# Two test-time-training/FFN layers on one core: rates turned on chip, the scan's first input and weights loaded a stage earlier, one FFN trip and one base product moved

## What is computed

```python
def step(carry, x):                       # scanned over 32 chunks of 16 tokens
    W1_s, b1_s = carry                    # one 16x16 state per head and sequence
    xq, xk, xv, eta_mb = x
    Z1 = xk @ W1_s + b1_s
    grad = _ln_fused_l2_bwd(Z1, xv - xk, ln_w, ln_b)
    Attn1 = jnp.tril(xq @ xk.swapaxes(-1, -2))
    b1_bar = b1_s - jnp.tril(eta_mb) @ grad
    Z1_bar = xq @ W1_s - eta_mb * Attn1 @ grad + b1_bar
    last_eta = eta_mb[:, :, -1, :, None]
    W1_new = W1_s - (last_eta * xk).swapaxes(-1, -2) @ grad
    b1_new = b1_s - jnp.sum(last_eta * grad, axis=-2, keepdims=True)
    out = xq + _ln(Z1_bar, ln_w, ln_b)
    return ((W1_new, b1_new), out)
...
ttt_lr_eta = jax.nn.sigmoid(ttt_lr).transpose(0, 1, 2, 4, 3) / HD      # the learning rates
...
hdn = jax.nn.silu((xf @ gate_w.T) * gate_s) * ((xf @ up_w.T) * up_s)   # the FFN, 512 -> 1408 -> 512
out = (hdn @ down_w.T) * down_s
```

## Time and profile before

| what | value |
|---|---|
| median of 3 runs | 2010.04 us (2007.79 to 2011.96) |
| profiled execution, its own time | 2006.43 us |
| its span, first to last instruction | 2004.8 us |
| mean granted TensorE clock | 0.981 |
| TensorE busy (PE) | 1875.6 us, 94% |
| VectorE, ScalarE, GpSimd busy | 1224.2, 979.8, 1022.7 us |

### The profile page before, as it was taken

How to read it: one execution, slowest core, us unless ns; L and a number is a source line. 1 busy time by engine, 2 the same in 40 slices (tenths; PEclk the granted TensorE clock), 3 DMA queues, 4 the chain that set the end, 5 groups by cost and what they waited for, 6 DMA issues and landing times. The chain is left out here.

```text
span 2004.8 us, 34531 instructions
## 1 busy us (share of the span) xinstructions
PE 1875.6 (94%) x12504; PEld 1414.9 (71%) x12504; DVE 1224.2 (61%) x2415; ACT 979.8 (49%) x2115; POOL 1022.7 (51%) x894
## 2 busy tenths in 40 slices
PE   5898999998999999799999989999999999999998
PEld 3676777666666665488778866777777777777776
DVE  4563566788788874467344456666666666666663
ACT  3332556566665655445444335444444444444442
POOL 5444566556565654420243347555555555555552
PEclk9899999999999999989999999999999999999999
DMA  7785657436334533232789841222323233322320
GB/s 243 275 297 191 230 169 262 123 110 220 119 114 150 190 117 97 73 108 92 239 258 289 290 176 54 88 113 95 123 99 116 95 105 117 116 83 73 107 98 30
DMA packets 157111, 297.96 MB, mean 149 GB/s; under 512 B 20240, under 2 KB 97296, under 8 KB 150288
## 3 DMA queue, kind: packets, MB, share of 16 engines
q1 hardware_dynamic: 155856, 294.70, 43.7%
q10 hardware_dynamic: 1088, 1.05, 0.2%
HBM read 221.52 MB, written 74.19 MB: 148 GB/s over the span
## 5 line engine op out<-in xcount | busy, mean ns | idle before, releaser
L2005 POOL TENSOR_SCALAR probs<-probs,rsum 128x512 f32<-128x512 f32 x256 | 396.1, 1565 | 249.0 <-DVE rsum L2141 249.0
L2105 ACT ACTIVATE p_tok<-bank 128x512 fp32r<-128x512 f32 x256 | 154.5, 606 | 346.4 <-PE bank L2045 346.3
L2137 DVE TENSOR_REDUCE nmax<-bank 128x1 f32<-128x512 f32 x256 | 158.9, 683 | 95.2 <-PE bank L2037 95.2
L2147 DVE TENSOR_TENSOR p_tok<-bank,p_tok 128x512 fp32r<-128x512 f32 x256 | 173.3, 680 | 16.1 <-ACT p_tok L2105 16.1
L2097 ACT ACTIVATE probs<-bank,nmax 128x512 f32<-128x512 f32 x256 | 172.8, 692 | 3.2 <-DVE nmax L2137 3.2
L60 PE MATMUL bank<-xs,ffn_w 128*128 128x512 f32 x352 | 152.9, 434 | 6.7 <-issue 3.4
L2045 PE MATMUL bank<-ident,probs 128*128 128x128 f32 x1024 | 156.5, 277 | 2.8 <-DVE p_tok L2147 2.8
L1493 POOL TENSOR_TENSOR y_pieces<-y_tok,y_pieces 128x512 fp32r<-128x512 f32 x48 | 66.1, 1393 | 181.9 <-ACT y_pieces L1698 181.9
L2045 PEld LDWEIGHTS bank<-ident,probs 128*128 128x128 f32 x1024 | 122.3, 141 | 51.1 <-issue 27.5
L61 PE MATMUL bank<-xs,ffn_w 128*128 128x512 f32 x352 | 138.8, 394 | 0.0
L62 PE MATMUL bank<-xs,ffn_w 128*128 128x512 f32 x352 | 138.6, 394 | 0.0
(11 more groups left out here) (281 smaller groups left out, 4951.4 us busy)
## 6 DMA issues: line engine op xcount, KB each, us to landing
ffn_w<-ffn_pieces SPq DMA_DIRECT2D x120, 512.0 KB, 3.8
uvo<-uvo_pieces SPq DMA_DIRECT2D x15, 2048.0 KB, 8.6
wq<-wq_pieces SPq DMA_DIRECT2D x16, 1536.0 KB, 6.5
ffn_pieces<-stage SPq DMA_DIRECT2D x30, 512.0 KB, 4.1
xs<-xn_pieces SPq DMA_DIRECT2D x4, 2048.0 KB, 8.1
y_tok<-in_gup SPq DMA_DIRECT2D x32, 256.0 KB, 3.6
wk<-wk_pieces SPq DMA_DIRECT2D x16, 512.0 KB, 3.6
ffn_w<-ffn_pieces SPq DMA_DIRECT2D x16, 384.0 KB, 3.5
```

Of the source, the lines that this page charges most:

```text
L2005: nc.gpsimd.tensor_scalar(probs[:, u % 8, :], probs[:, u % 8, :], rsum[:, u % 8:u % 8 + 1], None, ALU.mult).then_inc(norm_done, 1)
L2105: nc.scalar.activation(p_tok[:, Q % 2, 0, :, hh * P:(hh + 1) * P], banks[4 + u % 2][:].rearrange("p (k q) -> p k q", k=NBLK), ACT.Copy).th ...
L2137: nc.vector.tensor_reduce(nmax[:, u % 8:u % 8 + 1], banks[u % HG][:], axis=X_AXIS, op=ALU.max, negate=True).then_inc(max_done, 1)
L2147: nc.vector.tensor_tensor(p_tok[:, Q % 2, 1, :, q], banks[4 + u % 2][:].rearrange("p (k q) -> p k q", k=NBLK), p_tok[:, Q % 2, 0, :, q].bi ...
```

## The change

1. **Rates.** `move_rates` and its scratch are gone. `pick_rates` on TensorE, between the V and Q projections of the last tile, makes 64 matmuls with 0/1 matrices (`pick`, a new constant that SP loads into the dead `x_sb`), which turn `lr_raw` into the layout of `lr` in bank 5; one VectorE copy takes it to `lr`. The division by HD runs after the second V job instead of after the fourth.
2. **First input and weights.** `xs` and `ffn_w` get the addresses of the K and V weights of the projection stage. SP loads the first `xs` when the K jobs of the last tile are done; ScalarE's queue loads the first four FFN weight tiles at the end of its program, when the V jobs are done. The scan stage's SP queue then starts with `cst`.
3. **First trips.** TensorE runs the first four trips of the FFN at the start of the scan stage, ahead of `turn_k(0)`; step 0 has seven in its first place instead of eleven.
4. **Table.** In steps 9 to 31 one trip moves from the fourth place of a step to the first.
5. **Order.** The second `scores` of a step stands ahead of `base`.

```diff
-                    def move_rates():
-                        sp.wait_ge(sig_done, 2)
-                        for b in range(BATCH):
-                            sp.dma_start(lr_dram[b].rearrange("(m n) t e x -> (n t) m (e x)", m=NF), lr_raw[:, NF * b:NF * b + NF, :]).then_inc(lr_out, 16)
-                        sp.wait_ge(lr_out, 16 * BATCH)
-                        for b in range(BATCH):
-                            for e in range(2):
-                                c = 32 * b + 16 * e
-                                sp.dma_start(lr[c:c + 16, :, :], lr_dram[b].rearrange("n t e x -> t e n x")[:, e, :, :]).then_inc(lr_in, 16)
+                    def load_first_xs():
+                        sp.wait_ge(job_ready, JT * (NTB - 1) + NF)
+                        sp.wait_ge(xs_out, 32)
+                        sp.dma_start(xs[:].bitcast(F32), xs_pc[0]).then_inc(xs_in, 16)
...
+                        if t == NTB - 1:
+                            sp.wait_ge(xc_done, NF * NTB)
+                            sp.dma_start(x_sb[:, 0, :], A["pick"]).then_inc(pick_in, 16)
+                            load_first_xs()
...
-                    move_rates()
...
-                    sp.wait_ge(lr_in, 16 * 2 * BATCH)
...
+                    def pick_rates():
+                        pe.wait_ge(pick_in, 16)
+                        pe.wait_ge(sig_done, 2)
+                        pe.wait_ge(std_done, NTB)
+                        for c in range(P // CHUNK):
+                            for e in range(2):
+                                for b in range(BATCH):
+                                    ins = nc.tensor.matmul(banks[5][32 * b:32 * b + 32, c * NF * NX:(c + 1) * NF * NX], pick[:, c, e, :],
+                                                           lr_raw[:, NF * b:NF * b + NF, e * NX:(e + 1) * NX],
+                                                           start=(e == 0), stop=(e == 1), skip_group_check=True)
+                        ins.then_inc(picked, 1)
...
+                        if t == NTB - 1:
+                            pick_rates()
                         project(t, kinds(t)[2])
...
+                    act.wait_ge(job_ready, JT * (NTB - 1) + 2 * NF)
+                    for w in range(NEARLY):
+                        act.wait_ge(st_out[w % NST], 16 * (w // NST + 1))
+                        n = width(JOBS_T[w])
+                        act.dma_start(fw[:, w, :, 0:n, :].bitcast(F32), fw_pc[w][:, :, 0:n, :]).then_inc(fw_in[w], 16)
...
+                            if kind == kinds(t)[2] and t == NTB - 1:
+                                dve.wait_ge(picked, 1)
+                                nc.vector.tensor_copy(lr[:].rearrange("p (m c) x -> p c m x", m=NF),
+                                                      banks[5][:].rearrange("p (c m x) -> p c m x", m=NF, x=NX)).then_inc(picked_out, 1)
...
-            share = lambda n: (11, 3, 2, 2) if n < LAG else (8, 2, 2, 1) if n < NSTEP else (2, 2, 1, 1)
+            share = lambda n: (11, 3, 2, 2) if n < LAG else (9, 2, 2, 0) if n < NSTEP else (2, 2, 1, 1)
...
-                    load_xs(0)
-                    load_fw(0)
                     load_cst(0)
-                    for j in range(1, NWP):
+                    for j in range(NEARLY, NWP):
                         load_fw(j)
...
+                    for x in range(NF):
+                        trip(x)
                     turn_k(0)
...
                         ffn(n, 2)
+                        if ps:
+                            scores(ps[1])
                         G = opens_at(n)
                         if G is not None:
                             base(G)
-                        if ps:
-                            scores(ps[1])
                         ffn(n, 3)
```

More of the change, by code:

```diff
@@ L559, in build @@
             s = sb_in(st)
[L560 to L562 removed]
+            LAG = 9
+            s("home_of_xs_and_fw", [P, 36 * 256])
             hid_hi, hid_lo = s("hid_hi", [P, 4, TB], F32R), s("hid_lo", [P, 4, TB], F32R)
@@ L601, in build @@
             grad_out = [sem("ttt_grad_out0"), sem("ttt_grad_out1")]
-            fw_in = [sem(f"ttt_fw_in{i}") for i in range(NWP)]
             NPART = NSUPER * NF * BATCH
@@ L824, in ffn, with trip @@
-                            if k == w - 1:
-                                ins.then_inc(f_ready, 1)
+                            if x >= NF:
+                                trip(x)
+                    def trip(x):
+                        j, k = TRIPS[x]
+                        t, kind, a, o = JOBS[j]
+                        w = trips[j]
+                        bank = fb[j % 2]
+                        if k == 0:
+                            pe.wait_ge(fw_in[j % NWP], 16 * (j // NWP + 1))
+                            if j >= 2:
+                                pe.wait_ge(ev_sem[kind_of(j - 2)], nth(j - 2) + 1)
+                            if kind == "gate":
+                                pe.wait_ge(xs_in, 16 * (t + 1))
+                        if kind == "down" and o < 2:
+                            pe.wait_ge(hlo_done, NI * t + THIRDS[a][0] + k + 1)
+                        wh, wl = fw[:, j % NWP, 0, k, :], fw[:, j % NWP, 1, k, :]
+                        if kind == "down":
+                            xh_, xl_ = hid_hi[:, k, :], hid_lo[:, k, :]
+                        else:
+                            xh_, xl_ = xs[:, 0, k, :], xs[:, 1, k, :]
+                        ins = exact_matmul(nc, bank[:], wh, wl, xh_, xl_, start=(k == 0), stop=(k == w - 1))
+                        if k == w - 1:
+                            ins.then_inc(f_ready, 1)
```

49 lines of the change are left out of this document (17 added, 32 removed).

## The result

The changed kernel takes 1995.57 us (median of 4, 1992.11 to 1999.45) beside 2009.30 for the kernel before, run with it: ratio 0.9926, 95% interval 0.9902 to 0.9949. That is 14.9 us less by the ratio and 13.7 by the two medians; 8.4 were forecast. The profiled execution took 1999.45 us, its span is 1997.6 at a mean clock of 0.985. TensorE is busy for 1870.6 us, still 94%.

The account below looks back on a forecast made before the run. TensorE, busy 94% of the span, was taken as the bound, so gains come from its gaps or clock. Terms 7.0 + 3.7 - 1.0 - 1.3 = 8.4 us gave a forecast of 2001.6 us, range 1994.5 to 2006.5.

Parts of the forecast that it names:

- Seam: Parts 1 to 3, between projection and scan stage: a gain of 7.0 us, with 3.4 and 8.6 as ends.
- 208.8 forecast: Sign at the scan's start: the first state update comes near 208.8 us (205 to 213), before at 215.84.
- clock of the window: Sign: the mean clock over 195 to 216 us rises above 0.85, from 0.69 before.
- 194.0 forecast: Start of the scan stage: its first transfer goes at 194.0 us instead of 194.91, a gain of 0.9.
- The picks: 64 small matmuls on TensorE before the last Q projection: they cost 1.3 us.
- a sign that it would fail: At the scan's start: the forecast is wrong if the first trip waits for `ffn_w`.
- up to 3.5 us late: End of the projection stage: six FFN stores queue behind the early `xs` load, making the gain up to 1 us less.
- Table: Part 4, a trip moved in the scan's steps: 3.7 us gained by an earlier product, less 1.0.
- -1.0: Table, steps 10, 14, 18 and 30: GpSimd's work moves forward and slows VectorE's gradient; 1.0 us lost, 4.0 at most.
- +3.7 for the product's lead: `z_product` 0.68 us earlier shortens TensorE's waits at steps 10, 11, 12, 20, 22, 28, 30: 3.7 us, ends zero and 7.8.
- Behind finishing steps: Scan steps after a finishing step: VectorE works through, so an earlier product gains nothing there.
- Order: Part 5, second scores ahead of `base`: the snapshots of steps 15 and 23 wait for `base`, 1.3 us lost in all.

Follow-up runs that it names:

- e5: The kernel before, run and profiled again with nothing changed: 2008.50 us, ratio 0.9999.
- e3: The changed kernel with only the old order restored (base ahead of the second scores), so seam and new table: 1994.63 us, ratio 0.9927.
- e4: The changed kernel with only the old table (8, 2, 2, 1) restored, so seam and new order: 1999.51 us, ratio 0.9949.
- e6: The changed kernel, run and profiled again: 1994.94 us, ratio 0.9932.
- e1: The changed kernel with the old table and the old order, so parts 1 to 3 alone: 2002.69 us, ratio 0.9962.
- e7: The kernel before with part 1 alone: rates turned on chip, all loads at the stage's start, no first trips: 2008.17 us, ratio 0.9999.
- e8: The kernel before with parts 2 and 3 alone: early loads and four first trips, rates still through DRAM: 2011.89 us, ratio 1.0008.
- e9: e1 with the evictions of jobs ending in the fourth place moved to the third, TensorE's order unchanged: 1996.12 us, ratio 0.9944.
- e10: e3 with the evictions of jobs ending with the 13th trip held back in the fourth place: 1999.92 us, ratio 0.9962.
- e12: e11 with base ahead of the second scores at steps 15 and 23 only: 2004.48 us, ratio 0.9979.
- e2: The kernel before with the new table and new order alone, without the seam: 1998.89 us, ratio 0.9954.
- e13: e3 with the table (10, 2, 1, 0) instead of (9, 2, 2, 0) in steps 9 to 31: 2001.48 us, ratio 0.9965.
- e14: e3 with the table (10, 1, 2, 0) instead of (9, 2, 2, 0) in steps 9 to 31: 2005.39 us, ratio 0.9980.
- e11: The changed kernel with the first four weight tiles loaded by SP behind its six stores, instead of by ScalarE: 2003.59 us, ratio 0.9982.

## Why the prediction was right or wrong

**Seam: right, 7.0 forecast, 7.6 (ratio) and 7.0 (trace) measured.** `state_update(0)` 208.83 (208.8 forecast), clock of the window 1.00 (above 0.85). That the stage starts at 194.05, with 194.0 forecast, is luck: it starts between 192.80 and 195.85 in the nine profiles of kernels with the whole seam, 193.31 in e5. The picks took 1.99 us of TensorE and not 1.3. The medians bound the seam by 4.4 and 7.6 us. The first trip waited 1.80 for weights, which the forecast named as a sign that it would fail; it didn't, since VectorE's setup (`w_x` ready at 197.96) took as long as the wait, the four trips and `turn_k` (198.13). In e3 it was 4.1 us, the clock fell and the state update came at 212.6; over the nine profiles it comes between 207.7 (e4) and 212.6. The wait alone doesn't decide it: e6 waited 3.04 without a low stretch (208.82), e1 2.08 with one (211.8). The six stores behind the early `xs` took 9.86 us to issue instead of 7.62, and ScalarE's `cst` stores began 10.6 us behind the first of them instead of 8.6. e7 (7.70 and 8.4, no early load) and e8 (9.86 and 10.6, early load, no picks) show that the load does it. By the rule of the Trainium skill, "DMA: Bandwidth & Descriptors", section "Queues, rings and completion order", that each DMA engine takes a queue's descriptors in order, the stores were to come up to 3.5 us late; the trace agrees that `cst` comes some 2 late. Whether the queue's order or the shared engines do it, no run tells.

**Table: the step that failed.** For the evictions the forecast wrote "in steps 10, 14, 18 and 30 such work moves forward; [...] I take -1.0". These are steps in which a job ends with the ninth trip. The jobs that end with the thirteenth (steps 10, 14, 18, 22, 26 and 30) it took at nothing: that trip moves from the fourth place to the third, and with it the eviction jumps over the next step's square, square root and table reload on ScalarE, 6.3 us at step 19. GpSimd's work thereby moves out of VectorE's last operations. In place of -1.0 the runs showed +3.0 us for these evictions alone (e9 against e1) and +4.9 on top of the new table (e3 against e10): the term had the wrong sign. The table gave 5.7 us by the traces in place of 3.7 - 1.0.

The sign could have been read from the trace of before. The earlier trace rows show 0.92 for 0.42 at step 16, where no job ends in the fourth place before it and where the table gained nothing (19.83 and 19.79 us). At step 19 the same trace has four slow operations in a row, of which this is the first:

```profile
527.30 0.97 DVE L1149 SCALAR_TENSOR_TENSOR t<-st,gx_gt_xh 128x256 f32<-128x256 f32 x1
```

The Trainium skill's "SBUF — State Buffer", section "SBUF: two separate sides", has such a VectorE operation and a GpSimd operation shut each other out; the trace agrees that it is slower beside GpSimd (0.98 against 0.43).

**The +3.7 for the product's lead is off too.** The steps that it named gave 2.9, but by luck: step 11 gave 1.38, twice the 0.68 that an earlier product can give, and steps 10 and 22 0.16 and -0.45 where 0.68 and 0.51 were forecast. Steps 15, 19, 23 and 27, set at nothing, gave 4.1; 17, 21 and 25 lost 1.6; the rest gave 0.2. With the evictions held back (e10) the lead is worth 0.8 in all. The sentence "Behind finishing steps VectorE works through [...] and an earlier product gains nothing" held for the product: in e10 steps 15, 19, 23 and 27 together gave 0.4. The forecast also took a trip at 0.68 us wherever it stands, and the one that moved had cost 0.90.

**What the table lost.** In steps 17 and 25 TensorE waits 1.59 and 1.67 at L60 (0.33 and 0.34 in e1): that trip needs a bank whose eviction stands behind ScalarE's square root and table load. At step 17 TensorE now is there 10.3 us after the last state update instead of 11.2 (487.19 - 1.59 - 475.27; e1: 487.38 - 0.33 - 475.86), while the chain on VectorE, busy with `pt` behind a finish, frees the bank no earlier: TensorE goes on 11.9 us behind the state update, and 11.5 in e1. That the product's lead is given back here is the likely reading, not a shown one: e10 has the same waits (1.65 and 1.67), and no run takes them away alone.

**Order: -1.3 forecast, 0 by the medians**, inside what can be told. The snapshots do wait more (5.7 us in e6, 4.8 in e3), but e12 shows that giving that back buys nothing. At equal clock steps 8 to 30 are 2.4 us longer in e6 than in e3; the medians don't show them, and they don't lie where the forecast put its cost: steps 15, 16, 23 and 24 are together within 0.1 us of e3's, steps 10, 13 and 29 are 1.6 longer.

**Sum.** By e1, e3 and e6, 7.6 + 7.0 + 0 = 14.6, against 14.9 at first and 13.7 in e6; e2 shows that the split is good to some 3 us. What is missing from 8.4 is above all the table: 4.3 of the 6.5 us by the medians, 3.0 by the trace, 1.3 the order, 0.6 the seam. The traces explain less than the medians: in e6 7.0 to the first state update, 376.5 - 373.3 = 3.2 in steps 8 to 30 at equal clock and 0.6 to the second layer, 10.8 in all. What is left, 3 to 4 us, can be chance: layer 2, whose code is the same, is 1154.5 to 1161.8 us long in the profiled executions, with 27 to 42 us at low clock. The six with the new order had 33 us of it in the mean, the others 38; whether that is more than chance stays open. The range, 1994.5 to 2006.5, held the time.

## What to carry to other kernels

When a table moves a trip from one place to another, follow the job that ends with it: its eviction moves to another place in another engine's program, past whatever stands there. Write down for each place what the eviction is ahead of and behind (a table reload, a copy on the chain), and price that jump, not the trip's length. e3, e13 and e14 differ by one trip, and e14 lies 11 us above e3. Add what a lone trip between small matmuls costs over one in a row.

Before prefetching into a block's end, look at which small transfers decide that end. Here the early loads were worth nothing or cost time while the round trip of the rates was there (e8), and lost their worth again when they ran ahead of the last stores (e11). And count the stages from an event of the same execution: the stage start itself moved by 1.6 us between two profiles of one kernel.

## What was not expected of the hardware

Eight small read-backs took 4.04 and 5.79 us in the two profiles of the kernel before and 11.53 beside 2 MB of weight loads from another queue (e8). A stage that starts 3.25 us later loses 5.2, with 6.8 us more of low clock (e11). The clock's low stretches of 3.4 us come at places that differ from one execution to the next, 1.6 us each. They are most of the ±5 us between single executions of one kernel: over the 215 timed executions of the experiments and of the kernel before beside them, each taken against the mean of its group, the time falls as the mean granted clock rises, with a correlation of -0.85.
